# Two-part attention: centring the projection weights instead of the projections

## The reference

```python
def _ln(t, w, b):
    m = jnp.mean(t, axis=-1, keepdims=True)
    v = jnp.var(t, axis=-1, keepdims=True)
    return (t - m) * jax.lax.rsqrt(v + EPS) * w + b
...
kv_dca = (y_dca @ Wkv_dca + bkv_dca).reshape(b, DCA, 2, H, HD)
k_dca = _ln(kv_dca[:, :, 0], kn_dca_w, kn_dca_b)
...
q = _ln((x @ Wq + bq).reshape(b, s1, H, HD), qn_w, qn_b)
kv = jnp.concatenate([y_main @ Wk + bk, y_main @ Wv + bv], axis=-1)
kv = kv.reshape(b, s2, H, 2 * HD)
k = _ln(kv[..., :HD], kn_w, kn_b)
v = kv[..., HD:]
...
ctx = ctx + DCA_WEIGHT * ctx_dca
return ctx @ Wo + bo
```

## Time and profile before

| | us |
|---|---|
| runs (3) | 1888.89, 1889.65, 1890.13; median 1889.65 |
| the profiled execution | 1889.1 |
| its span, first to last instruction | 1886.5 |
| mean granted TensorE clock | 0.909 of full speed |
| projection block | 942.58 to 964.31 |
| normalising block | 964.70 to 992.66 |
| attention loop's start | 992.98 |

### The profile page before, as it was taken

One profiled execution on the slowest core, in us unless ns is written; L12 is line 12 of the kernel. 1 busy time (PEld: TensorE's weight loads), 2 busy tenths in 40 slices (PEclk: granted clock), 3 DMA queues, 4 the chain that ended last, 5 costly groups with the idle time before them and its releaser, 6 DMA issues. The chain is left out here.

```text
span 1886.5 us, 30002 instructions
## 1 busy us (share of the span) xinstructions
PE 1558.5 (83%) x10985; PEld 1125.0 (60%) x11033; DVE 1357.4 (72%) x2235; ACT 827.7 (44%) x1284; POOL 488.4 (26%) x531
## 2 busy tenths in 40 slices
PE   6899999999798888366667778889998678888864
PEld 5678888888794665122355534578776335646631
DVE  3289999999575864799678583557676843668688
ACT  3366766677332552533323421333334222525544
POOL 2234333433251421377304102210000000314200
PEclk9899999999899898688878979999999859898985
DMA  4000000000000001000010002010000310010000
GB/s 152 28 26 25 22 25 28 28 28 14 12 1 13 2 4 41 1 0 0 0 48 5 29 1 115 1 38 9 12 17 21 131 58 31 2 60 2 2 1 22
DMA packets 18148, 49.81 MB, mean 26 GB/s; under 512 B 2035, under 2 KB 8436, under 8 KB 16886
## 3 DMA queue, kind: packets, MB, share of 16 engines
q1 hardware_dynamic: 18038, 48.31, 7.5%
HBM read 47.26 MB, written 1.05 MB: 26 GB/s over the span
## 5 line engine op out<-in xcount | busy, mean ns | idle before, releaser
L2184 DVE SCALAR_TENSOR_TENSOR arena<-psum,arena 128x1016 f32<-128x1016 f32 (+2 forms) x240 | 303.6, 1265 | 35.7 <-ACT arena L2121 30.0
L903 DVE TENSOR_REDUCE limits<-psum 128x4 f32<-128x512 f32 (+2 forms) x256 | 148.1, 620 | 81.9 <-PE psum L758 49.3
L2030 PE MATMUL psum<-ssm_XT_hi,ssm_split 128*128 128x512 f32 x640 | 194.4, 406 | 11.7 <-POOL ssm_split L1989 5.6
L871 ACT ACTIVATE PT<-psum 128x1024 f32<-128x1024 f32 x112 | 108.6, 1021 | 115.2 <-PE psum L789 115.2
L2030 PEld LDWEIGHTS psum<-ssm_XT_hi,ssm_split 128*128 128x128 f32 x640 | 116.1, 191 | 37.0 <-POOL ssm_split L1989 10.8
L2121 ACT ACTIVATE arena<-psum,arena 128x1024 f32<-128x1024 f32 x80 | 89.1, 1114 | 105.8 <-PE psum L2030 104.4
L758 PE MATMUL psum<-K,QR 32*128 32x256 f32 (+1 forms) x320 | 118.4, 442 | 9.0 <-DVE limits L903 6.5
L2875 POOL TENSOR_TENSOR fed<-dtx,b_all 128x1024 f32<-128x1024 f32 x32 | 103.1, 3241 | 65.1 <-DVE state L2944 33.4
L1988 POOL TENSOR_TENSOR ssm_split<-arena,const 128x256 fp32r<-128x256 f32 x80 | 58.4, 730 | 198.9 <-PE psum L2030 196.1
L2944 DVE TENSOR_TENSOR_SCAN state<-decay,fed 128x1024 f32<-128x1024 f32 x32 | 103.1, 3261 | 6.8 <-POOL fed L2875 5.2
L2030 PE MATMUL psum<-ssm_XT_lo,ssm_split 128*128 128x512 f32 x320 | 101.0, 397 | 0.0
(11 more groups left out here) (483 smaller groups left out, 3721.3 us busy)
## 6 DMA issues: line engine op xcount, KB each, us to landing
expert_mask<-in_expert_masks SPq DMA_DIRECT2D x32, 256.0 KB, 2.9
arena<-in_ssm_in SPq DMA_DIRECT2D x16, 384.0 KB, 2.9
arena<-in_L_xattn SPq DMA_DIRECT2D x1, 5120.0 KB, 16.0
arena<-in_ssm_in SPq DMA_DIRECT2D x16, 256.0 KB, 3.0
arena<-in_L_ffn SPq DMA_DIRECT2D x1, 2592.0 KB, 8.7
arena<-in_L_xattn SPq DMA_DIRECT2D x2, 1280.0 KB, 10.4
arena<-in_L_ffn SPq DMA_DIRECT2D x1, 2176.0 KB, 9.0
ssm_gated<-in_ssm_z SPq DMA_DIRECT2D x4, 512.0 KB, 6.3
```

What stands on the lines that cost most here:

```text
L871: nc.scalar.activation(PT[:, u % 2, 2 * k:2 * k + 2, :, :].rearrange("p r h q -> p (r h q)"), p.psum[:, (2 + 2 * k) * 512:(4 + 2 * k) * 51 ...
L903: ins = nc.vector.tensor_reduce(limits[:, u % 2, r, :, k], score_bank(r)[:, :].rearrange("p (h k) -> p h k", h=4)[:, :, lo:hi], AX.X, ALU. ...
L2030: ins = nc.tensor.matmul(bank[tile_bank(r, tile) + half][:, :], w_part(tile, kw, c), x_part(kx, c, slice(half * 512, (half + 1) * 512)), s ...
L2184: ins = nc.vector.scalar_tensor_tensor(out[:, :, ago:], product[:, :, :P - ago], tap, out[:, :, ago:], ALU.mult, ALU.add)
```

## The change

The weights and biases of the query and key projections are centred per head in place, in the arena, by VectorE inside the projection block: `wq` before TensorE's first projection, `bq` before the first query copy, `wk`, `wk_dca` and `bk` between the query copies. The projections then need no centring, and the 128 x 2048 sums and subtractions are gone. ScalarE squares each tile of 128 x 512 as soon as it is copied; VectorE sums the squares of a tile (128 x 512) between later copies, in the projection block too, with the first square root and reciprocal. The normalising block scales by the deviation in eight instructions of 128 x 512, and a group of transposes waits for its own pair of batches only. The eight holding matmuls of that block are gone; three stand ahead of the first projection. The sums of the weights' magnitudes and their scale move behind the other work of that block.

```diff
+                        if kind == "q" and k == 0:
+                            hold_clock(p, bank[7], 3)
+                            pe.wait_ge(s.query_weights.sem, s.query_weights.at(0))
                         if kind == "k" and k == 0:
                             pe.wait_ge(s.operands_ready.sem, s.operands_ready.at(0))
+                            pe.wait_ge(s.key_weights.sem, s.key_weights.at(0))
...
+                @block.scalar
+                def _(act):
+                    for n in range(B):
+                        two = slice(2 * (n % 4), 2 * (n % 4) + 2)
+                        act.wait_ge(s.tile_out_dve.sem, s.tile_out_dve.at(n))
+                        nc.scalar.activation(square[n // 4][:, two, :], raw[n // 4][:, two, :], ACT.Square).then_inc(s.squared.up(), 1)
+                        if n == 5:
+                            act.wait_ge(s.moments_ready.sem, s.moments_ready.at(0))
+                            nc.scalar.activation(var[:, 0, :], var[:, 0, :], ACT.Sqrt).then_inc(s.deviation_ready.up(), 1)
...
+                    def centre(a):
+                        of_head = a.rearrange("p (h n) -> p h n", n=hd)
+                        heads = of_head.shape[1]
+                        then(nc.vector.tensor_reduce(mean[:, :heads], of_head, AX.X, ALU.add))
+                        then(nc.vector.tensor_scalar(mean[:, :heads], mean[:, :heads], 1.0 / hd, None, ALU.mult))
+                        return nc.vector.tensor_tensor(of_head, of_head, mean[:, :heads].rearrange("p (h o) -> p h o", o=1).broadcast_to([P, heads, hd]),
+                                                       ALU.subtract)
+
+                    def spread_of(n):
+                        two, k = slice(2 * (n % 4), 2 * (n % 4) + 2), n // 4
+                        dve.wait_ge(s.squared.sem, s.squared.at(n))
+                        then(nc.vector.tensor_reduce(var[:, k, n % 4 * 2 * H:(n % 4 + 1) * 2 * H], square[k][:, two, :].rearrange("p b (h n) -> p (b h) n", h=H),
+                                                     AX.X, ALU.add))
...
+                    centre(p.w("wq")).then_inc(s.query_weights.up(), 1)
+                    dve.wait_ge(s.query_weights.sem, s.query_weights.at(0))
+                    then(centre(p.w("bq")))
                     for n, (kind, k) in enumerate(tiles):
...
+                        if n == 0:
+                            then(centre(p.w("wk")))
+                        elif n == 1:
+                            centre(p.w("wk_dca")).then_inc(s.key_weights.up(), 1)
+                            dve.wait_ge(s.key_weights.sem, s.key_weights.at(0))
+                            then(centre(p.w("bk")))
+                        elif n == 3:
+                            spread_of(0)
+                            spread_of(1)
+                        elif n == 4:
+                            spread_of(2)
+                            spread_of(3)
+                            moments(0)
+                        elif n == 6:
+                            spread_of(4)
+                        elif n == 7:
+                            spread_of(5)
+                            dve.wait_ge(s.deviation_ready.sem, s.deviation_ready.at(0))
+                            then(nc.vector.reciprocal(var[:, 0, :], var[:, 0, :]))
+                        elif n == 9:
+                            spread_of(6)
+                        elif n == 10:
+                            spread_of(7)
+                            moments(1)
...
-                    for k in range(2):
-                        then(nc.vector.tensor_reduce(mean[:, k, :], grouped(raw[k]), AX.X, ALU.add))
-                        then(nc.vector.tensor_scalar(mean[:, k, :], mean[:, k, :], 1.0 / hd, None, ALU.mult))
-                        nc.vector.tensor_tensor(grouped(raw[k]), grouped(raw[k]), wide(mean, k), ALU.subtract).then_inc(s.centred.up(), 1)
...
+                    for j in range(B // 2):
+                        by_deviation(0, j)
+                    dve.wait_ge(s.deviation_ready.sem, s.deviation_ready.at(0))
+                    then(nc.vector.reciprocal(var[:, 1, :], var[:, 1, :]))
+                    for j in range(B // 2):
+                        by_deviation(1, j)
...
-                    pe.wait_ge(s.deviation_ready.sem, s.deviation_ready.at(0))
-                    hold_clock(p, bank[1], 8)
                     for n in range(8):
                         k, j = divmod(n, B // 2)
-                        pe.wait_ge(s.x_ready.sem, s.x_ready.at(k))
+                        pe.wait_ge(s.x_ready.sem, s.x_ready.at(n))
...
+                    pe.wait_ge(s.oT_ready.sem, s.oT_ready.at(0))
+                    pe.wait_ge(s.sums_ready.sem, s.sums_ready.at(0))
+                    nc.tensor.matmul(bank[0][:, 0:3], p.c("ones"), ternary.sums[:, :], start=True, stop=True).then_inc(s.spread_ready.up(), 1)
```

More of the change, by code:

```diff
@@ L952, in two_part_attention @@
             square = [sb2("square_q", [P, B, D]), sb2("square_k", [P, B, D])]
-            mean = sb2("mean", [P, 2, B * H])
+            mean = sb2("mean", [P, DC * H])
             var = sb2("var", [P, 2, B * H])
@@ L1034, in _ @@
-                    dve.wait_ge(s.spread_ready.sem, s.spread_ready.at(0))
-                    then(nc.vector.tensor_scalar(ternary.inv[:, :], bank[0][:, 0:3], 1.0 / (HID * D), 1e-5, ALU.mult, ALU.max))
-                    nc.vector.reciprocal(ternary.scale[:, :], ternary.inv[:, :])
-                    for k in range(2):
-                        dve.wait_ge(s.squared.sem, s.squared.at(k))
-                        then(nc.vector.tensor_reduce(var[:, k, :], grouped(square[k]), AX.X, ALU.add))
-                        nc.vector.tensor_scalar(var[:, k, :], var[:, k, :], 1.0 / hd, 1e-6, ALU.mult, ALU.add
-                                                ).then_inc(s.moments_ready.up(), 1)
@@ L1042, in _, with by_deviation @@
-                    for k in range(2):
-                        dve.wait_ge(s.deviation_ready.sem, s.deviation_ready.at(k))
-                        then(nc.vector.reciprocal(var[:, k, :], var[:, k, :]))
-                        dve.wait_ge(s.centred.sem, s.centred.at(k))
-                        nc.vector.tensor_tensor(grouped(raw[k]), grouped(raw[k]), wide(var, k), ALU.mult).then_inc(s.x_ready.up(), 1)
+                    def by_deviation(k, j):
+                        two = raw[k][:, 2 * j:2 * j + 2, :].rearrange("p b (h n) -> p (b h) n", h=H)
+                        factor = var[:, k, 2 * j * H:(2 * j + 2) * H].rearrange("p (h o) -> p h o", o=1).broadcast_to([P, 2 * H, hd])
+                        nc.vector.tensor_tensor(two, two, factor, ALU.mult).then_inc(s.x_ready.up(), 1)
@@ L1054, in _ @@
                                                         ALU.mult, ALU.add)
+                    dve.wait_ge(s.spread_ready.sem, s.spread_ready.at(0))
+                    then(nc.vector.tensor_scalar(ternary.inv[:, :], bank[0][:, 0:3], 1.0 / (HID * D), 1e-5, ALU.mult, ALU.max))
+                    nc.vector.reciprocal(ternary.scale[:, :], ternary.inv[:, :])
                 @block.scalar
                 def _(act):
+                    nc.scalar.activation(var[:, 1, :], var[:, 1, :], ACT.Sqrt).then_inc(s.deviation_ready.up(), 1)
+                    for j in range(B // 2):
+                        act.wait_ge(s.xT_psum.sem, s.xT_psum.at(j))
+                        dst, src = transposed(0, j)
+                        for b in range(2):
+                            ins = nc.scalar.activation(dst[:, b], src[:, b], ACT.Identity, scale=scaled[:, 0:1], bias=scaled[:, 1:2])
+                    ins.then_inc(s.oT_ready.up(), 1)
                     act.wait_ge(s.weights_loaded.sem, p.weights_total)
@@ L1061, in _ @@
                     ins.then_inc(s.sums_ready.up(), 1)
-                    for k in range(2):
-                        act.wait_ge(s.centred.sem, s.centred.at(k))
-                        nc.scalar.activation(square[k][:, :, :], raw[k][:, :, :], ACT.Square).then_inc(s.squared.up(), 1)
-                    for k in range(2):
-                        act.wait_ge(s.moments_ready.sem, s.moments_ready.at(k))
-                        nc.scalar.activation(var[:, k, :], var[:, k, :], ACT.Sqrt).then_inc(s.deviation_ready.up(), 1)
-                    for j in range(B // 2):
-                        act.wait_ge(s.xT_psum.sem, s.xT_psum.at(j))
-                        dst, src = transposed(0, j)
-                        for b in range(2):
-                            nc.scalar.activation(dst[:, b], src[:, b], ACT.Identity, scale=scaled[:, 0:1], bias=scaled[:, 1:2])
                 @block.tensor
                 def _(pe):
-                    pe.wait_ge(s.sums_ready.sem, s.sums_ready.at(0))
-                    nc.tensor.matmul(bank[0][:, 0:3], p.c("ones"), ternary.sums[:, :], start=True, stop=True).then_inc(s.spread_ready.up(), 1)
-                    pe.wait_ge(s.deviation_ready.sem, s.deviation_ready.at(0))
-                    hold_clock(p, bank[1], 8)
```

(2 more changed lines are left out.)

7 lines of the change are left out of this document (4 added, 3 removed).

## The result

| | before | changed |
|---|---|---|
| runs (6 each) | 1885.33 to 1890.22, median 1889.27 | 1879.82 to 1883.02, median 1881.63 |
| profiled execution, its span | 1889.1, 1886.5 | 1882.02, 1880.0 |
| mean granted TensorE clock | 0.909 | 0.910 |

The ratio is 0.9962, 95% interval 0.9953 to 0.9972: the change makes the kernel faster by about 7.2 us, 0.4%. The forecast was 1876.6, a gain of 13.0, with a range of 1873.5 to 1880.0. The sign was right, the size and the range were not.

A forecast was written before the change was run, and what follows sets the result against it. TensorE was taken to bound the projection block, VectorE's serial chain the normalising block. Normalising -16.42, projection +2.89 and GpSimd +0.5 gave -13.0 us, forecast 1876.6, range 1873.5 to 1880.0.

The forecast's parts named there:

- The normalising block: Second block: removing centrings, sums of squares and one reciprocal from VectorE leaves 11.54 of 27.96 us, -16.42.
- The shadow in the projection block: Projection block: of about 12.9 us of added VectorE work, 10 fall into holes or under the late start; +2.89.
- the working: Projection block: tile-by-tile queue of VectorE's copies, centrings and sums, ending the block at 967.20 instead of 964.31.
- Rival 4: Projection block: holes don't take the work, all 12.9 us lengthen it; gain only 3.5, 1886.1; chance 0.03.
- The term for GpSimd: Start of projection block: GpSimd's work beside wq's centring slows VectorE; +0.5, moving its whole chain.
- The sentence on the Trainium skill's lock: Start of projection block: under an exclusive port lock, scaling waits for a copy, subtraction meets only a memset; +0.2 instead of +0.5.
- My worst-case bound: Start of projection block: wq's subtraction waits for GpSimd's end, TensorE starts at 946.3; +2.0.
- rival 1: Projection block: GpSimd holds up wq to its end, or small centring instructions cost more; 1878.1; chance 0.12.
- rival 5: Projection block: waiting for wq drops TensorE's clock, projections run at half of it; slower, 1896.3; chance 0.02.
- The sign given for a wrong forecast: Profile, projection block: a first block under 23 or over 26 us would show the forecast wrong.
- Rival 2: Attention loop: starts colder, nine holding matmuls between the first scores cost 0.45 each; +2.0, 1878.6; chance 0.10.
- rival 3: Gains more: GpSimd costs nothing and the attention loop's lowered-clock stretch falls elsewhere; 1874.5; chance 0.07.

The follow-up runs named there:

- the thirteen holds: Changed kernel with 13 holding matmuls instead of 3 ahead of the first projection, GpSimd as it is; median 1878.95, ratio 0.9942.
- the kernel that centres early: Changed kernel with all centring moved into the sublayer in front, no holding matmuls or wait ahead of the projections; median 1874.94, ratio 0.9924.
- the kernel with the copies later: Changed kernel with only GpSimd's two context copies waiting for wq, its clears and small copies at once; run once, 1882.26.

## Why the prediction was wrong, point by point

- **The normalising block: right.** -16.42 forecast, -16.56 measured (27.96 to 11.40). The spacings, the order of what comes out behind VectorE, and the margin of ScalarE's chain (0.4 forecast, 0.5 measured) all held.
- **The shadow in the projection block: right.** Without the two disturbances the block takes 24.80 us; the working gave 24.6. The order of the queue, the sums in the holes and VectorE falling behind from the first v copies on show in the trace; the holes ahead of the seventh and eighth tile (T6 and T7 in the working) took up the 1.0 us by which GpSimd made the first copy late. Rival 4 did not happen.
- **The term for GpSimd: the step that failed first.** I took +0.5 from a cast's 0.2 to 0.3 us. It was +1.6. The cast in the earlier trace rows met the end of one product; wq's scaling met a copy and two clears without a gap between them. The sentence on the Trainium skill's lock (SBUF — State Buffer, "SBUF: two separate sides") had the right rule, but who goes next in a queue was my own assumption: I let the scaling slip in when the copy ended at 943.53, and the earlier trace rows show a clear following at once; the scaling waited until all clears were through (944.42), and the subtraction then met the copy. My worst-case bound, +2.0, held it, and so did rival 1, which had that price and a chance of 0.12.
- **The holding matmuls: a price at the wrong clock.** "Its three holding matmuls fill 1.3 us" used the half-clock price. At full clock they took 0.81 (0.27 each). By itself this cost nothing: with GpSimd out of the way the hole was 0.88 us, inside the 0.4 to 0.9 on which rival 5 was dismissed, and the clock stayed full. With the longer centring it was 2.46.
- **The clock: put at nothing, measured at 2.7.** Rival 5 had the mechanism, but let the clock fall for the whole block (+20.96) or not at all. It fell for the first 5.5 us of TensorE's work: +2.7 (the thirteen holds). My evidence against it, that in 966 to 968 the clock was still full more than 2 us after the last matmul, was read as a margin. In the changed kernel it fell between 944.40 and 944.80, within 1.4 us of the last hold's end at 943.45; before the change it fell at the end of the second row below, more than 4 us after the last matmul (the copy that it releases starts at 963.62). How long TensorE has been idle doesn't alone tell when its clock falls, so a row with one gap bounds nothing for another place. The sign given for a wrong forecast, a first block over 26 us, came true. The changed kernel, then the kernel before:

```profile
944.40:944.80 0.40, 0.00 (x0) 0.00 (x0) 0.37 (x2) 0.00 (x0) 0.40 (x2) 0.77 0.36 131
```

```profile
968.00:968.50 0.50, 0.00 (x0) 0.00 (x0) 0.50 (x1) 0.50 (x1) 0.00 (x0) 0.96 0.00 0
```

- **The loop: taken over unchanged at 70.55, measured at 72.31.** Rival 2 had a colder start, priced at +2.0, and I gave it 0.10. Its sign came half true: of the nine holding matmuls between the first scores, four ran at 0.47 us each and five at 0.25. That 1.8 measured is near its 2.0 is in part luck: the start accounts for 0.4 to 1.1 of it, and the rest was lost around a half-clock stretch 46 us into the loop; a stretch that falls elsewhere stood in rival 3 alone, as a gain. Nor is the reason that rival 2 gave, the longer pause before the loop, borne out. Before the change the last transposes ended 3.5 us before the loop's first holds, in the changed kernel 4.3, with only the small ones product between; in the kernel that centres early it was 5.1, and its loop took 70.55. So why the changed kernel started colder is open.
- **Behind the loop: 0.8, in no term and no rival.** 0.5 in the output stage, where the clock was 0.90 instead of 1.00, and 0.3 further on, with the same mean clock of 0.94 in both kernels. The cause was not tried; in the kernel with the copies later the output stage took 14.25 at a clock of 1.00, so the clock is not all of it.
- **The range.** Rivals 1 and 2, 1.5 and 2.0 us on the slow side, were taken as alternatives, each against a range that held one. Most of the first, a part of the fifth and the time of the second came together: with what was lost behind the loop, 1.1 + 2.7 + 1.8 + 0.8 is 6.4.

## What to carry to other kernels

Work put in front of TensorE's first matmul of a block can be paid twice: for its own length, and for the clock that falls meanwhile. Here waits of 1.80, 2.45 and 2.46 us behind three holding matmuls were, and one of 0.88 was not. Look for a place in an earlier block where the engine is idle and the data already there (here 13 us, which took 6.1 us of centring for nothing), and otherwise cover the whole wait with holding matmuls, counted at the full-clock price. A short one-input scaling in SBUF that comes up beside a queue of GpSimd instructions can wait for several of them and not for one (here each time through two clears); where the order is free, put GpSimd's clears beside a VectorE wait or beside copies out of PSUM. And a loop with the same code can differ by 1 to 3 us between two kernels, so compare stages before a change of this size is put down to an edit.

## What the runs showed of the hardware

- A one-input scaling of 32 or 16 values took 0.17 to 0.18 us alone, 1.09, 1.10 and 1.43 when it came up before two clears that followed a copy without a gap (it ended 0.02 to 0.04 us behind the second each time), and 0.53 beside a copy; a two-input subtraction of 512 took 0.69 with nothing beside it and 1.35 beside a copy; a reduction of 512 took 0.69 beside a clear and a copy.
- GpSimd's last copy took 0.76 in the changed kernel instead of the 0.29 of the earlier trace rows and ended just behind VectorE's subtraction (946.01 and 945.85). The subtraction had waited for the first of the two copies only, although the second followed without a gap. So a queue is not always waited for to its end; what decides it, no run shows.
- TensorE's clock fell within 1.4 us of the last matmul in the changed kernel, while before the change it was still full in 966 to 968, up to 4.4 us after it. A wait of 0.30 us behind 2.96 us of holds left it full, and so did one of 0.88 behind 0.81.
- The four transposes of a pair of batches took 0.8 us at half clock (3.12 us for sixteen), and nobody waited for them behind the first: the lowered clock there cost nothing, as the forecast said.
